# A gated linear-attention layer on one core: key shares first, value halves third and last, gates to tokens by 4-byte DMA, memory ahead of the output projection

## What is computed

```python
# 1. gated linear attention, 8 heads of 64
h = x * rsqrt(mean(x * x) + 1e-6) * norm_w
q, k, v = rope(heads(h @ Wq.T)), rope(heads(h @ Wk.T)), heads(h @ Wv.T)
beta, ig, og = sigmoid(h @ Wg.T + bg)          # one value per token and head
M = M * beta[t] + ig[t] * scale * outer(k[t], v[t])
y[t] = (q[t] @ M) * og[t]
x = layernorm(x + y @ Wout.T + bout)
# 2. memory over the 256 tokens of a sequence
r = 0.9 * r + (ctx * ctx)[t]
x = layernorm(x + x * r)
# 3. eight experts, each with its own tokens
x = layernorm(x + gelu(xn @ w1[e] + b1[e]) @ w2[e] + b2[e])
```

## Time and profile before

| | us |
|---|---|
| median of 3 runs | 1307.37 (1307.25 to 1307.8) |
| profiled execution, its own time | 1312.74 |
| span in the profile | 1310.9 |
| TensorE busy | 1273.4 |
| VectorE busy | 737.8 |
| POOL busy | 749.6 |
| ScalarE busy | 462.3 |

### The profile page before, as it was taken

One profiled execution on the slowest core, in us unless ns is written; L12 is line 12 of the kernel. 1 busy time (PEld: TensorE's weight loads), 2 busy tenths in 40 slices (PEclk: granted clock), 3 DMA queues, 4 the chain that ended last, 5 costly groups with the idle time before them and its releaser, 6 DMA issues.

```text
span 1310.9 us, 19484 instructions
## 1 busy us (share of the span) xinstructions
PE 1273.4 (97%) x6850; PEld 1033.8 (79%) x6850; DVE 737.8 (56%) x1273; ACT 462.3 (35%) x629; POOL 749.6 (57%) x518
## 2 busy tenths in 40 slices
PE   8899999999999999899999999999999999999998
PEld 7677887888887778668888888888788888888886
DVE  6868888888888888762343343343333423433324
ACT  5222333333222322262533534443334335334330
POOL 4566666766666666548437547375284385374561
PEclk9899999999999999899999999999999999999999
DMA  8544555555555444545307115135044062071220
GB/s 289 148 122 139 152 151 153 153 155 152 155 152 149 126 142 118 167 139 190 123 0 264 64 50 216 64 114 206 13 152 177 0 247 82 1 264 65 83 78 33
DMA packets 132613, 172.08 MB, mean 131 GB/s; under 512 B 13693, under 2 KB 75981, under 8 KB 132557
## 3 DMA queue, kind: packets, MB, share of 16 engines
q1 hardware_dynamic: 132556, 171.30, 40.5%
HBM read 137.44 MB, written 17.05 MB: 118 GB/s over the span
## 4 chain that ended last, share of the span: by engine, by line
PE 56%; DVE 2%; issue 1%; POOL 0%; ACT 0%; POOLq 0%; DVEq 0%
PE v_ps L86 5%; PE qk_ps L88 5%; PE v_ps L88 5%; PE qk_ps L87 4%; PE qk_ps L86 4%; PE v_ps L87 4%; PE gate_ps L87 4%; PE gate_ps L88 4%; PE gate_ps L86 4%; PE s_ps L86 2%; PE s_ps L88 2%; PE s_ps L87 2%; PE y_ps L86 2%; PE y_ps L87 2%; PE y_ps L88 2%; PE turn L1450 1%
## 5 line engine op out<-in xcount | busy, mean ns | idle before, releaser
L928 POOL TENSOR_TENSOR w_lo<-w_raw,w_hi 128x2048 fp32r<-128x2048 f32 x31 | 143.4, 4626 | 72.8 <-ACT w_hi L702 72.8
L920 POOL TENSOR_TENSOR w_lo<-w_raw,w_hi 128x2048 fp32r<-128x2048 f32 x32 | 147.9, 4620 | 10.6 <-ACT w_hi L712 10.6
L86 PE MATMUL qk_ps<-xT_parts,wqkv_hi 128*128 128x256 f32 x512 | 150.6, 294 | 0.9 <-DVE wqkv_lo L966 0.8
L1199 DVE CAST hid_hi<-gate_ps 128x512 fp32r<-128x512 f32 x62 | 42.9, 692 | 190.9 <-ACT gate_ps L735 184.6
L1010 DVE TENSOR_TENSOR_SCAN decays<-f_all,diag 128x384 f32<-128x384 f32 x128 | 149.0, 1213 | 0.6
L88 PE MATMUL qk_ps<-xT_parts,wqkv_lo 128*128 128x256 f32 x512 | 145.6, 284 | 0.0
L87 PE MATMUL qk_ps<-xT_parts,wqkv_hi 128*128 128x256 f32 x512 | 145.2, 284 | 0.0
L1199 DVE CAST hid_hi<-v_ps 128x512 fp32r<-128x512 f32 x62 | 42.9, 692 | 176.2 <-ACT v_ps L735 176.2
L892 POOL TENSOR_TENSOR rstd_b<-mean_var_b,ln_eps_b 128x4 f32<-128x4 f32 x15 | 3.7, 245 | 215.4 <-DVE mean_var_b L1184 215.4
L837 POOL TENSOR_TENSOR rot<-rot 128x256 f32<-128x256 f32 x64 | 65.3, 1021 | 81.0 <-DVE rot L1037 80.8
L735 ACT ACTIVATE gate_ps<-gate_ps,b_cols 128x512 f32<-128x512 f32 x64 | 42.2, 659 | 192.7 <-PE gate_ps L88 192.7
(11 more groups left out here) (218 smaller groups left out, 3185.5 us busy)
## 6 DMA issues: line engine op xcount, KB each, us to landing
w_raw<-in_w SPq DMA_DIRECT2D x64, 1024.0 KB, 7.4
f_all<-f_dram SPq DMA_DIRECT2D x16, 1024.0 KB, 4.8
qkT<-rot SPq DMA_DIRECT2D x256, 64.0 KB, 2.0
xT_raw<-in_xT SPq DMA_DIRECT2D x16, 512.0 KB, 10.6
x_both<-in_x SPq DMA_DIRECT2D x16, 512.0 KB, 9.8
f_all<-f_dram SPq DMA_DIRECT2D x16, 512.0 KB, 5.9
c_both<-in_ctx_in SPq DMA_DIRECT2D x16, 512.0 KB, 11.2
x_dram<-res SPq DMA_DIRECT2D x16, 512.0 KB, 11.9
```

The source lines that it names most:

```text
L86: eng.matmul(out, lhs_hi, rhs_hi, start=first, stop=False)
L920: pool.tensor_tensor(w2_lo[s % 2][:], w2_raw[s % 2][:], w2_hi[s % 2][:].bitcast(F32), ALU.subtract)\
L928: pool.tensor_tensor(w1_lo[s % 2][:], w1_raw[s % 2][:], w1_hi[s % 2][:].bitcast(F32), ALU.subtract)\
L1199: dve.tensor_copy(high, up_ps[c % 2][:]).then_inc(hid_hi_done, 1)
```

## The change

What it does, part by part:

1. From step 2 on turn_gates is dropped. `store_f` stores 16 gate rows instead of 8, and SP's new `load_g` reads the input gates back with tokens on the partitions, by two DMAs of 128 x 8 elements of four bytes. token_gates takes them from g_raw.
2. From step 2 on the order of shares is k, k, v half 0, q, q, v half 1.
3. VectorE's order follows: token_gates and gate_v(b, 0) stand in slot 6, behind weigh and rope_parts(2); gate_v(b, 1) stands at the end; rope_parts are in slots 2, 3, 6, 7; slot 5 has four scans, slot 7 one, and one is at the end.
4. cross_memory(b-1) stands ahead of project_out(b-1).
5. store_o and spread_o on SP and o_row on POOL stand at the end of the body before; POOL makes o_tables ahead of both rotations.
6. Step 0: the low part of Wout is made by POOL in one operation, not by VectorE in four; four scans go to step 1. SP's order in body 0 differs.
7. Last steps: the statistics of the first expert's tokens are taken in slot 4 of body 15 (before: slots 1 and 2); two of the turned tiles use the v_ps and gate_ps banks; scores(15, 0) waits for two low tiles, not four.

```diff
-SCANS = {3: (0, 1), 5: (2, 3, 4), 7: (5, 6, 7)}
+SCANS = {3: (0, 1), 5: (2, 3, 4, 5), 7: (6,)}
-SHARES = ((2, 0), (1, 0), (1, 1), (2, 1), (0, 0), (0, 1))
+FIRST_SHARES = ((2, 0), (1, 0), (1, 1), (2, 1), (0, 0), (0, 1))
+SHARES = ((1, 0), (1, 1), (2, 0), (0, 0), (0, 1), (2, 1))
...
+            def load_g(b):
+
+                rows = f_dram[b.odd, NH * L:2 * NH * L].rearrange("(h t) -> t h", t=L)
+                for j in range(NT):
+                    sp.dma_start(g_raw[:, j, :], rows[j * P:(j + 1) * P, :], allow_slow_non_contiguous=True).then_inc(g_in, 16)
...
                     store_f(b + 1)
+                    store_o(b + 1)
                     spread_f(b + 1)
+                    load_g(b + 1)
+                    spread_o(b + 1)
...
             def token_gates(b):
-                dve.wait_ge(gates_turned, b.after(1, 1))
+                if b.n <= 1:
+                    dve.wait_ge(gates_turned, b.after(1, 1))
+                else:
+                    dve.wait_ge(g_in, (b - 2).after(16 * NT, 16 * NT))
...
+                    if b.within(B) and n == 2 and b.n >= 2:
+                        rope_parts(b, 0)
...
+                    if b.within(B) and n == 3 and b.n >= 2:
+                        rope_parts(b, 1)
+                        clear_f(b)
+                    if b.within(B) and n == 6 and b.n >= 2:
+                        rope_parts(b, 2)
+                        token_gates(b)
+                        gate_v(b, 0)
+                    if b.within(B) and n == 7 and b.n >= 2:
                         rope_parts(b, 3)
...
+                if b.within(B) and b.n >= 2:
+                    gate_v(b, 1)
...
                 if (b + 1).within(B):
                     gate_products(b + 1)
+                if (b - 1).within(B) and b.n != B:
+                    cross_memory(b - 1)
                 if (b - 1).within(B):
                     project_out(b - 1)
...
-                if (b - 1).within(B) and b.n != B:
-                    cross_memory(b - 1)
```

More of the change, by code:

```diff
@@ L184, in layer_program @@
     g_tok = sb("g_tok", [P, NT, NH])
+    g_raw = sb("g_raw", [P, NT, NH])
     o_rows = sb("o_rows", [NG, L])
@@ L307, in layer_program, with token_bank @@
     minus_one = sb("minus_one", [P, NM])
+    def token_bank(e, k):
+        if e.i is None and e.n == 0 and k >= 2:
+            return up_ps[k - 2]
+        return turn[k % 2]
     acc = [y_ps, s_ps, qk_ps[:, 0:D], qk_ps[:, D:2 * D]]
@@ L382, in store_f @@
                 sp.wait_ge(gates_done, b.after(1, 1))
-                sp.dma_start(f_dram[b.odd].rearrange("(h t) -> h t", h=NH), gates[0:NH, :]).then_inc(f_stored, 16)
+                sp.dma_start(f_dram[b.odd].rearrange("(h t) -> h t", t=L), gates[0:2 * NH, :]).then_inc(f_stored, 16)
             def spread_f(b):
@@ L663, in body @@
                         square_ctx(b - 1)
-                    if (b - 2).within(B) and b.n <= B and c == 0:
+                    if (b - 2).within(B) and b.n <= B and c == (2 if b.n == B else 0):
                         scale_x2(b - 2)
@@ L874, in body @@
                 if b.within(B) and b.n >= 1:
+                    rotate(b, 0)
                     rotate(b, 1)
@@ L1087, in body @@
                 for n in range(NH):
-                    if (b - 2).within(B) and b.n <= B and n == (b.n == B):
+                    if (b - 2).within(B) and b.n <= B and n == (3 if b.n == B else 0):
                         add_memory(b - 2)
@@ L1094, in body @@
                     if b.n == 1 and n == 0:
-                        scan(b - 1, 6)
-                        scan(b - 1, 7)
-                    if b.n == 1 and n == 0:
                         o_row(b)
+                        for m in range(2, 6):
+                            scan(b - 1, m)
                     if b.n == 0 and n == 2:
@@ L1101, in body @@
                         rope_parts(b, 1)
-                    if b.within(B) and n == 2:
+                    if b.within(B) and n == 2 and b.n <= 1:
                         token_gates(b)
                         gate_v(b, 0)
+                    if b.within(B) and n == 2 and b.n >= 2:
+                        rope_parts(b, 0)
+                    if b.n == 1 and n == 2:
+                        scan(b - 1, 6)
+                        scan(b - 1, 7)
                     if (b - 1).within(B) and b.n != B and n in (3, 5, 7):
@@ L1139, in body @@
                     y_low(b - 1, KC - 1)
-                if b.within(B) and b.n != 0:
+                if b.n == 1:
                     rope_parts(b, 3)
+                if b.within(B) and b.n >= 2:
+                    gate_v(b, 1)
                 if b.n == -1:
@@ L1147, in body @@
                     sum_gates(b + 1)
+                if b.within(B) and b.n != 0:
+                    scan(b, NH - 1)
                 if b.n == B:
@@ L1156, in body, with token_stats @@
                     norm_stats(b - 1, 0)
-                if b.n == 0:
-                    for m in range(2, 6):
-                        scan(b, m)
-            def token_stats(ms):
+            def token_stats():
                 dve.wait_ge(x2_in, 16)
-                for m in ms:
+                for m in range(NM):
                     dve.bn_stats(e_stats[0][:, m, :], x2[:, m, :]).then_inc(e_stats_done[0], 1)
```

115 lines of the change are left out of this document (59 added, 56 removed).

## The result

The changed kernel takes 1384.6 us (1379.45 to 1386.83, 4 runs) against 1307.59 before: ratio 1.0566, 95% interval 1.0535 to 1.0597. I had forecast slower, at 1343.4 us, with a range up to 1361. The sign and the place are right and the size is not: 77.0 us more where I had 36.0. The profiled execution took 1379.45, so the two traces differ by less: 66.8 us of span.

The account below looks back on a forecast made before the run. TensorE, busy for 97% of the span, was taken as the bound. Steps 2 to 14 +40.7, start −2.4, step 15 −0.6 and stage end −1.7 gave +36.0 us on a 1307.37 median: 1343.4 us, range up to 1361.

Parts of the forecast that it names:

- It stalls 2.65 us in every step: TensorE before v's half 1 in slot 6, waiting for gate_v(b, 0): 4.30 us chain less 1.65 us of work; bounds 2.4 to 3.5.
- the deciding point: The stall before v's half 1 at which the change would neither gain nor lose over 13 steps: 1.2 us.
- By my count they end at the very time at which scores(3) is readable: VectorE's four scans in slot 5, 4.84 us together, were to end just in time for weigh(6), adding no lateness.
- token_gates' 0.48: Link of VectorE's slot 6 chain ahead of gate_v(b, 0): the pair of token_gates was priced at 0.48 us.
- the half clock: TensorE at 1.2 GHz behind the v's half 1 stall: 1.7 us lost in three steps of four, 17 us over 13 steps.
- some 0.75 us: TensorE's wait at scores(1) for VectorE's chain behind the output projection, each step; bounds 0.4 and 1.1.
- the start: Bodies 0 and 1: one 1.98 us stall and its 1.7 clock loss gone, 1.3 of new waits: −2.4 us, from −8 to +1.
- the end's 1.1: Forecast for the last steps: step 15 −0.6 us, and scores(15, 0) no longer waiting for all four turned tiles −1.7.
- Rival 1: The stall is 2.65 us in each step but no half clock follows: +19.0, 1326 us; chance 0.20.
- Rival 2: Faster: gate_v(b, 0) isn't late, so slot 6 has no stall and turn_gates' cost goes: 1292 us; chance 0.07.
- Rival 3: The 4-byte gate loads delay o_dram's load, output tables and rope_parts(2), 1.5 us more a step: 1363 us; chance 0.08.
- Rival 4: About even with the kernel before, from a stall near 1.2 us before v's half 1; chance 0.03.

Follow-up runs that it names:

- gate_slot4: The changed kernel with token_gates and gate_v(b, 0) moved from slot 6 to slot 4 of VectorE's body: 1302.78 us.
- two_scans: The changed kernel with two scans in VectorE's slot 5 and three in slot 7, instead of four and one: 1361.88 us.
- gate_before_rope: The changed kernel with rope_parts(b, 2) behind token_gates and gate_v(b, 0) in slot 6, instead of ahead of them: 1344.45 us.
- fill_wait: The changed kernel with 30 unread products put ahead of TensorE's wait before v's half 1, from step 2 on: 1356.56 us.
- before_with_load_g: The kernel before with only load_g on SP in place of turn_gates from step 2 on, token_gates still in slot 2: 1313.65 us.
- turn_kept: The changed kernel with the gates brought to tokens by turn_gates on TensorE in slot 2 as before, and no load_g: 1376.28 us.
- slot4_memory_behind: gate_slot4 with SP's body 0 order and step 0's scans as before, and cross_memory behind project_out in all steps: 1287.3 us.

## Why the prediction was right and wrong

**Right: what decides.** "It stalls 2.65 us in every step" at v's half 1, behind scores(3), released by gate_v: the stall stands there in all 14 steps, and gate_slot4 shows that it is VectorE's order alone. Without the stall the change is faster than before, as the forecast had it; the deciding point, a stall of 1.2 us, was not tested.

**Wrong: the size of the stall,** the term 2.65 (bounds 2.4 to 3.5). It measured 4.32 on average, outside the bounds. Two links of its chain were priced too low.
- "By my count they end at the very time at which scores(3) is readable": they end 1.05 us later; two_scans took exactly that away. The four scans aren't what was too dear: they took 4.48, less than the 4.84 that I had given them. I had priced the first pair of scans of the step by nothing new, and it takes 3.78 us here (248.68). In the trace of before the pair takes 2.29 in most steps. The change had moved POOL's tables ahead, by the earlier spread_o, and with the rotation behind them they now stand beside the pair:

```profile
248.47 1.29 POOL L850 TENSOR_TENSOR rot<-rot,rope_sb 128x512 f32<-128x512 f32 x1
249.72 1.93 POOL L851 TENSOR_TENSOR rot<-rot,rope_sb 128x512 f32<-128x512 f32 x1
251.61 1.38 POOL L858 TENSOR_TENSOR rot<-rot 128x256 f32<-128x256 f32 x1
```

The trace of before had the two prices side by side: the three scans of slot 5 take 2.64 us with POOL idle (first line), and 3.68 in a step where POOL's tables run beside them (236.22 to 240.04).

```profile
268.28 2.64 DVE L1010 TENSOR_TENSOR_SCAN decays<-f_all,diag 128x384 f32<-128x384 f32 x3
235.27 3.68 DVE L1010 TENSOR_TENSOR_SCAN decays<-f_all,diag 128x384 f32<-128x384 f32 x3
```

That the scans end late is shown by an experiment; that POOL is why is read from such rows, and no run moved POOL's tables by themselves.

- token_gates' 0.48 was taken from a row with POOL idle. Here it runs beside POOL's rotation and takes 1.08 us from its start to gate_v's. gate_before_rope, where it runs with POOL idle, has 0.47 again.

The stall is 1.67 us above the forecast on average, which makes 21.7 us over 13 steps.

**Wrong: the half clock,** "three steps of four" at 1.7 us. For a stall of 2.65 that was near: gate_before_rope, with 2.55, has it in 7 of 12 steps. But a stall of 4.3 has it in every step and at times for twice as long: 1.9 us a step by fill_wait, where I had 1.3. That is another 7.7 us over 13 steps. I had read the 5.34 us stall of before as followed by the short stretch; it was followed by the long one. The Trainium skill ("TensorE: Matmul & The Clock Gate", HAM oscillation) names gaps above about 3.4 us as those that bite; here 2.55 us did in 7 cases of 12 and 3.27 us in 11 of 12, so the measurement decides and the trace of before was no exception.

**Wrong, the other way: scores(1),** "some 0.75 us". It waits 0.27 to 0.41 by distance, 0.37 on average (idle 0.34 in the trace below), 4.9 us less over 13 steps. add_memory was quicker (1.88 to 2.22 us, 2.72 in the earlier trace rows's step), the low bound that I had given.

```profile
243.83 0.49 PE L1384 MATMUL turn<-qkT 64*128 64x128 f32 x4 [0.34 <-DVE probs L1066]
```

**Wrong in sign: the start,** "−2.4, from −8 to +1": +4.7. I saw that scans leave body 0, but not that spread_f, now SP's last there, waits for them (step 0's last scans end at 51.75 us, and its load is issued at 51.90, with two large loads already under way).

From third to last start of the gates' products the trace shows +63.3 where I had +40.7; the three terms above (21.7 + 7.7 − 4.9 = 24.5) are that difference of 22.6 to 2 us. These I can't place; part of it is that my 440.4 was a stretch cut elsewhere, and these starts are 445.1 apart in the trace of before. With the start's 7.1 and the end's 1.1 (−1.2 measured, −2.3 forecast) the 36.0 become the 66.8 of the two spans. The medians lie 10 us further apart than the profiled executions, because that of before was at the higher end of its runs (1312.74) and that of the change the lowest (1379.45); I take both as they are.

**The rivals.** Rival 1 (the clock holds) is refuted here: it never holds behind 4.3 us. At a stall of the forecast size it would have been half right: gate_before_rope keeps the clock in 5 steps of 12. Rival 2 is what gate_slot4 is: the change without the late gate_v. Rival 3 is refuted for this kernel: SP does issue the two loads for 3.92 us a step, and they land some 6 us on, but nothing waits for them in slot 6. With token_gates in slot 2 it would be true, as before_with_load_g shows. Rival 4 (about even) needed a stall near 1.2 us, and no such stall came about. The Trainium skill ("DMA: Bandwidth & Descriptors", rules for kernel authors) has one descriptor per element for such a load; the trace agrees, with 29,247 more packets under 512 bytes (13,693 to 42,940), of which 14 steps of 2,048 elements would make 28,672; turn_kept, without the loads, has 13,820.

```profile
274.96 3.92 SPq L406 DMA_DIRECT2D g_raw<-f_dram  x2
```

## What to carry to other kernels

When a bank is freed by another engine, walk that engine's queue from the last thing that it must itself wait for: the release comes after the sum of everything written there, whatever is already computed, and moving two calls here was worth 82 us. Price each link by a row in which the other engines do what they will do after the change, and price what a moved step waits for before what waits for it. A wait that repeats costs more than its length: fill it or shorten it, and look at the clock behind it.

## What the runs showed of the hardware

- **VectorE beside POOL.** The same pair of token_gates took 0.99 us beside POOL's rotation and 0.47 with POOL idle (gate_before_rope); read from the gates' PSUM bank, it took 0.47 even while standing at the same place (turn_kept). A pair of scans took 3.78 us beside POOL's tables and 2.29 beside its rotation, and three scans took 2.64 with POOL idle. I had expected scans of 1.2 us whatever POOL does.
- **The clock behind stalls.** Equal stalls get unequal answers: stalls of 2.55 us were followed by 1.2 GHz in 7 of 12 steps (gate_before_rope), of 3.07 in 12 of 12 (turn_kept), of 3.27 in 11 of 12 (two_scans), of 4.3 in 12 of 12 and then at times for 5.9 us and more. The single wait of 1.9 us in step 3 of slot4_memory_behind was followed by none, where one of 1.98 was in the trace of before. So the length of a stall alone doesn't decide. Products whose result nobody reads, put into the wait, kept 2.4 GHz and saved 28 us (fill_wait).
